# A graph layer on one core: the dense and the picked edges' steps of each stage moved a group of gathers apart

## What is computed

```python
src = node_feature[edge_src]
parts = [relu(node_feature)]
for t in range(3):
    msg = relu(src @ W_e[t].T + b_e[t])
    msg = where(edge_type == t, msg, 0)
    parts.append(segment_sum(msg, edge_dst, num_segments=N))
agg = concatenate(parts, axis=1)
updated[node] = agg[node] @ W_n[type of node].T + b_n[type of node]
x = layernorm(x + (updated + x))
```

## Time and profile before

| what | value |
|---|---|
| device time, 3 runs | 922.02 us median (919.35 to 922.12) |
| the profiled execution | span 1076.0 us from its first to its last instruction |
| PE busy | 771.1 us, 72% |
| DVE busy | 683.5 us, 64% |
| POOL busy | 671.4 us, 62% |
| ACT busy | 149.6 us, 14% |
| mean granted clock of PE | 0.872 |
| main loop: first gather, last gather | 107.01 us, 1049.44 us |

### The profile page before, as it was taken

One profiled execution on the slowest core, in us unless ns is written; L12 is line 12 of the kernel. 1 busy time (PEld: TensorE's weight loads), 2 busy tenths in 40 slices (PEclk: granted clock), 3 DMA queues, 4 the chain that ended last, 5 costly groups with the idle time before them and its releaser, 6 DMA issues. The chain is left out here.

```text
span 1076.0 us, 13097 instructions
## 1 busy us (share of the span) xinstructions
PE 771.1 (72%) x4200; PEld 611.8 (57%) x4200; DVE 683.5 (64%) x1539; ACT 149.6 (14%) x397; POOL 671.4 (62%) x718
## 2 busy tenths in 40 slices
PE   5574267777778778777676686888787786778866
PEld 3242156666666566566555565666566565566654
DVE  7997866666555656656566565656656654465645
ACT  2264101101101101100110110011011001111101
POOL 7776655666566666665666665666666666665660
PEclk9697578978898998998999988989888978898898
DMA  7476312422222223223223223223223233132320
GB/s 219 135 256 190 81 50 60 86 72 67 78 80 75 71 77 85 72 70 89 71 70 93 74 67 91 71 67 96 72 67 108 71 105 90 45 93 70 87 57 16
DMA packets 65777, 94.03 MB, mean 87 GB/s; under 512 B 16497, under 2 KB 49233, under 8 KB 65711
## 3 DMA queue, kind: packets, MB, share of 16 engines
q0 software_dynamic: 22432, 45.99, 17.2%
q1 hardware_dynamic: 40577, 43.14, 13.0%
q10 hardware_dynamic: 2702, 4.08, 1.3%
HBM read 80.23 MB, written 12.92 MB: 87 GB/s over the span
## 5 line engine op out<-in xcount | busy, mean ns | idle before, releaser
L619 POOL DMA_INDIRECT tab<-message_table,idx_t x630 | 594.3, 943 | 353.0 <-issue 170.4
L1116 DVE TENSOR_TENSOR work<-key_t,ps 128x378 f32<-128x378 f32 (+1 forms) x180 | 109.5, 610 | 253.1 <-remote 133.0
L1516 PE MATMUL ps<-work,tab 128*128 128x126 f32 x1260 | 197.4, 304 | 35.4 <-DVE acc L1125 20.6
L1516 PEld LDWEIGHTS ps<-work,tab 128*128 128x128 f32 x1260 | 183.3, 219 | 50.3 <-DVE acc L1125 25.5
L1546 PE MATMUL ps<-we_t,order_f 128*128 128x128 f32 x540 | 115.4, 368 | 123.2 <-DVE order_f L1204 84.1
L1546 PEld LDWEIGHTS ps<-we_t,order_f 128*128 128x128 f32 x540 | 93.3, 255 | 135.6 <-DVE order_f L1204 88.8
L1595 PE MATMUL ps<-wn_t,stage 128*128 128x384 f32 x294 | 104.6, 493 | 0.0
L1204 DVE TENSOR_TENSOR order_f<-ps,dst_raw 128x768 f32<-128x768 f32 x45 | 43.1, 957 | 71.7 <-remote 56.7
L615 POOL DMA_INDIRECT xg<-in_x,esrc_t x67 | 71.0, 1060 | 23.9 <-issue 17.7
L1595 PEld LDWEIGHTS ps<-wn_t,stage 128*128 128x128 f32 x294 | 56.3, 193 | 39.7 <-issue 3.1
L747 ACT ACTIVATE dense_f<-ps 128x256 f32<-128x256 f32 x45 | 17.2, 383 | 432.7 <-PE ps L1548 228.8
(11 more groups left out here) (231 smaller groups left out, 952.2 us busy)
## 6 DMA issues: line engine op xcount, KB each, us to landing
tab<-message_table,idx_t POOLq DMA_INDIRECT x630
message_table<-tab SPq DMA_DIRECT2D x24, 384.0 KB
dst_raw<-dense_types SPq DMA_DIRECT2D x45, 192.0 KB
wn_raw<-message_table SPq DMA_DIRECT2D x22, 384.0 KB
src_wide<-dense_lists SPq DMA_DIRECT2D x45, 128.0 KB
xg<-in_x SPq DMA_DIRECT2D x11, 256.0 KB
work<-in_x ACTq DMA_DIRECT2D x10, 256.0 KB
out<-xg SPq DMA_DIRECT2D x10, 256.0 KB
```

Of the source, the lines that this page charges most:

```text
L619: pool.indirect_dma_start(msg[:, slot, :], None, table, bass.IndirectOffsetOnAxis(ap=rows, axis=0)).then_inc(signal, 16)
L1116: dve.tensor_tensor(hot[:, first:first + n, :].rearrange("p c (t w) -> p c t w", w=WIN), keys.broadcast_to((P, n, T, WIN)), iota_win.rearr ...
L1516: ins = pe.matmul(sums_bank(nth), msg[:, column, :], hot[:, column, :], start=(c == 0), stop=(c == n - 1))
```

## The change

The dense and the picked edges' steps are spread over the stage, so that a group of gathers lies between one engine's step and the next engine's answer. The main parts:

- `dense_turn(j+1)` goes from the end of stage j to behind the sum of group 1; DVE makes its one-hots a group earlier, and masks after group 2. `dense_make(j)` stays behind the sum of group 0 (its mask is now made in stage j-1).
- `dense_sum(j)` is cut in two: side 0 behind the sum of group 2, side 1 behind the sum of group 3. From stage 2 to 43 their results go to spare columns of the two `AGG` banks (`D_SUM_AT`), in place of the bank `DENSE_PS`.
- The picked edges' sum goes to spare columns of the second `AGG` bank (`E_SUM_AT`) and has no turn of its own. `early_make` moves one stage later, behind the sum of group 0, `early_select` behind group 1, `early_sum` behind the sum of group 3.
- Because a bank now holds several sums, DVE waits for all of them before it adds the group's (`add_group`); all adds count on one semaphore, `added`, with a table of their order (`adds_of`).
- `finish_h(j-2)` is done at the end of stage j, where before it was done as `finish_h(j-3)` after group 1 of stage j; the two-step finish of the extra tiles goes over two stages.
- SP loads the dense edges' data ahead of the self rows, and the first batch of tiles is two in place of one.

```diff
@@ constants @@
-E_XT_PS, E_MSG_PS = 5, (6, 7)
+E_MSG_PS, E_XT_AT = (6, 7), T * D
+E_SUM_AT, D_SUM_AT = P, 2 * P
+PEELED_DENSE = 2
@@ order of the adds @@
+        def adds_of(j):
+            if j == 0:
+                return ["g0", "g1", "g2", "g3"]
+            if j == 1:
+                return ["g0", "g1", "p0", "p1", "g2", "g3", "e", "d0", "d1"]
+            if j == NI - 1:
+                return ["g0", "g1", "g2", "d0", "d1", "g3"]
+            return ["g0", "g1", "g2", "d0", "g3"] + (["e"] if j <= NE else []) + ["d1"]
...
@@ DVE, stage 1 @@
+            def iteration_one():
+                bases_of = load_bases(1, True)
+                dense_mask(0)
...
+                dve.wait_ge(group_summed, NG + 2)
+                one_hot(2, 1)
+                add_group(1, 1, bases_of[1])
+                first_of = load_bases(0, False)
+                for side in range(SETS):
+                    dense_add(0, side, first_of[2 * side], added_by(1, "p" + str(side)))
+                early_select(0)
+                self_types()
+
+                dve.wait_ge(group_summed, NG + 3)
+                one_hot(2, 2)
+                add_group(1, 2, bases_of[2])
+                dense_mask(1)
+                dense_hot(1)
...
+                dense_onehot(2)
+                dense_mask(2)
@@ DVE, stages 2 to 43 @@
+                dve.wait_ge(group_summed, NG * j + 3)
+                one_hot(j + 1, 2)
+                dve.wait_ge(d_summed, SETS * j + 1)
+                add_group(j, 2, bases_of[2])
+                dense_add(j, 0, bases_of[0], added_by(j, "d0"))
+                dense_mask(j + 1)
...
+                dve.wait_ge(group_summed, NG * j + 4)
+                one_hot(j + 1, 3)
+                dve.wait_ge(d_summed, SETS * j + 2)
+                if early:
+                    dve.wait_ge(e_summed, j)
+                add_group(j, 3, bases_of[3])
...
@@ PE, stage 1 @@
+                sum_group(1, 2)
+                dense_make(1)
+
+                sum_group(1, 3)
+                early_sum(0)
+                early_turn(1)
+                for side in range(SETS):
+                    dense_sum(1, side)
+                spread_types()
+                dense_turn(2)
@@ PE, stages 2 to 43 @@
+                sum_group(j, 0)
+                if j <= NE:
+                    early_make(j - 1)
+                dense_make(j)
...
+                sum_group(j, 1)
+                dense_turn(j + 1)
+
+                sum_group(j, 2)
+                dense_sum(j, 0)
+                finish_linear(j - 2, first=j == 2)
+                finish_turn(j - 1, j - 1, loads)
...
+                sum_group(j, 3)
+                dense_sum(j, 1)
+                if j <= NE:
+                    early_sum(j - 1)
+                if j < NE:
+                    early_turn(j)
+                place_selfs(j - 1, j - 1)
```

More of the change, by code:

```diff
@@ L66 @@
 FIN = 2
-BEHIND = 2
+PEELED_DENSE = 2
 WIN = 42
@@ L1366, in _ @@
             dve.wait_ge(acc_zeroed, 1 + 1 + 1 + 1 + 8 + 8)
[L1367 to L1369 removed]
+            iteration_zero()
+            iteration_one()
+            for j in range(2, NI - 1):
+                iteration(j, extra_of(j), extra_of(j - 1))
                 if j == BAD_AT - 1:
@@ L1549, in dense_make, with dense_sum @@
                 ins.then_inc(d_made, 1)
-            def dense_sum(j):
+            def dense_sum(j, side):
                 pe.wait_ge(d_ready, j + 1)
                 pe.wait_ge(d_hot, j + 1)
-                for side in range(2):
-                    ins = pe.matmul(dense_sums(side), dsel[:, side, :], dhot[:, side, :], start=True, stop=True)
-                ins.then_inc(d_summed, 1)
+                pe.matmul(dense_sums(j, side), dsel[:, side, :], dhot[:, side, :], start=True, stop=True
+                          ).then_inc(d_summed, 1)
             def spread_types():
@@ new lines, in iteration_zero, with iteration_one @@
+            def iteration_zero():
+                sum_group(0, 0)
+                early_turn(0)
+                for g in range(1, NG):
+                    sum_group(0, g)
+                dense_keys()
+                dense_turn(0)
+            def iteration_one():
+                sum_group(1, 0)
+                early_make(0)
+                dense_make(0)
+                sum_group(1, 1)
+                for side in range(SETS):
+                    dense_sum(0, side)
+                finish_turn(0, 0, 1, first=True)
+                dense_turn(1)
+                sum_group(1, 2)
[3 more added lines that the diff above has]
+                early_turn(1)
+                for side in range(SETS):
+                    dense_sum(1, side)
+                spread_types()
+                dense_turn(2)
@@ new lines, in last_iteration @@
+            def last_iteration(j):
+                sum_group(j, 0)
+                dense_make(j)
+                finish_turn(ORDER[KE], KE, 2, 1)
+                sum_group(j, 1)
+                finish_linear(j - 2)
+                finish_turn(j - 1, j - 1, len(BATCHES))
+                sum_group(j, 2)
+                for side in range(SETS):
+                    dense_sum(j, side)
+                place_selfs(ORDER[KE], KE, 1)
+                linear_open(KE, 1)
+                place_selfs(j - 1, j - 1)
+                linear_open(j - 1)
+                sum_group(j, 3)
+                linear_types(j - 1, 0)
+                linear_types(KE, 1)
@@ L1694, in batches_up_to @@
                 return sum(first <= tile for first, _ in BATCHES)
-            iteration(0, True, False)
-            dense_keys()
-            dense_turn(0)
-            for j in range(1, NI - 1):
-                iteration(j, j < NE, extra=j - EXTRA_AT if EXTRA_AT <= j < EXTRA_AT + KE else None,
-                          loads=batches_up_to(j - 1))
-            iteration(NI - 1, last=True)
-            linear_types(KE, 1)
+            iteration_zero()
+            iteration_one()
+            for j in range(2, NI - 1):
+                iteration(j, batches_up_to(j - 1), extra_of(j), extra_of(j - 1))
+            last_iteration(NI - 1)
             pe.wait_ge(ctl_set, 1)
```

438 lines of the change are left out of this document (182 added, 256 removed).

## The result

| | before | after |
|---|---|---|
| device time, median | 921.79 us (917.42 to 924.42, 16 runs) | 923.78 us (921.27 to 929.51, 16 runs) |
| ratio to before | | 1.0036 (1.0020 to 1.0051) |
| the same, timed again later | 920.29 us (35 runs) | 924.23 us (12 runs), 1.0040 (1.0019 to 1.0061) |
| span of the profiled execution | 1076.0 us; a second one 916.8 us | 924.7 us; a second one 924.0 us |

The change makes the kernel 0.36 to 0.40% slower, about 3.5 us. The forecast was 920.5 and no measurable change; slower by over 0.3% had 0.20. The time lies in the range given, but the likeliest case had the wrong sign.

The account below looks back on a forecast made before the run. The prediction took POOL's nearly back-to-back gather issue to bound the timed kernel. Its terms summed as 922.0 − 1 + 0 + 3 − 3.5 = 920.5 us, own range 915 to 926, with a wider range from 900 to 927.

Parts of the forecast that it names:

- The bound: Whole timed loop: POOL issues gathers nearly back to back, 3.4 us of waits left; the profile's stage waits come with profiling.
- Rival A: POOL's gathers: timed pitch shorter than 1.248 us, so stage waits remain and the change takes them; 896.5 to 905.5 us, chance 0.26.
- Rival B: Stage loop: profile at face value, POOL's waits of 127.8 us scale to 109.5 and go; 812 us, chance 0.04.
- 107.0 + 785.0 + 26.6: Profile's time ahead of the first gather, 629 gather pitches, and time from the last gather's start: 918.6 us.
- Step 1: PE's waits for mask, esel and finish_linear, 4.9 us a stage, all go; hidden beside POOL when timed, so −1 us.
- Step 2: Shared PSUM banks: DVE waits for all sums, likeliest some 0.3 us twice a stage, covered by its spare time; cost 0.
- step 3: dense_turn and early_make moved on PE, dense-edge loads moved ahead on SP; busy times hold, cost 0.
- Step 4: Stages 1 to 2: the sum of group 3 slides behind dense_make(1), later waits absorb part; bounds +1.0 and +5.5, taken +3 us.
- Step 5: Last stage: a tile finished and mask made a stage earlier, removing PE's variance wait; 0 to 4.82 us, taken −3.5.

Follow-up runs that it names:

- a_start: The changed kernel with both stage-1 steps put back (a_order) and DVE's self_types moved to the end of stage 0: 918.59 us, ratio 0.9975 to before.
- b_start: The kernel before with only DVE's self_types moved from stage 1 to the end of stage 0: 919.11 us, ratio 0.9966.
- b_again: The kernel before, unedited, profiled a second time: span 916.8 us, median 918.6 us (1 run).
- a_back: a_order plus, in the last stage, the extra tile's place_selfs and linear_open a group earlier on PE: 920.86 us, ratio 0.9993 to before.
- after_again: The changed kernel, unedited, timed and profiled again: 924.23 us, ratio 1.0040 to before.
- b_turn: The kernel before with one step of the change alone, dense_turn(2) ahead of the sum of group 0 of stage 2: 924.35 us, ratio 1.0037.
- a_s13: The changed kernel with the sum of group 3 of stage 1 put back ahead of dense_make(1) on PE: 924.72 us, ratio 1.0053 to before.
- a_turn2: The changed kernel with dense_turn(2) put back behind the sum of group 0 of stage 2: 923.74 us, again 923.10; ratios 1.0049 and 1.0032 to before.
- a_order: The changed kernel with both put back, group 3's sum ahead of dense_make(1) and dense_turn(2) behind stage 2's group-0 sum: 922.16 us, ratio 1.0025 to before.

## Why the prediction was wrong

*The bound.* Right for the stages: POOL is at its floor there at 922, and the profile's 127.8 us of waits don't exist in the timed runs. The second profile of before and the two runs with fewer gathers show it. Rival A (a shorter pitch) is out: the pitch is 1.249 to 1.252 in the thirteen undisturbed traces with all 630 gathers. Rival B too. But that 107.0 + 785.0 + 26.6 came within 3.4 us of the median was luck. The undisturbed ends are 100.7 and 13.8 us, 19.1 shorter, and POOL waits 16.9 us over its gaps, all of it ahead of stage 5 (6.24 us at 132.84 and 7.03 at 165.77 above all): 100.7 + 785.4 + 16.9 + 13.8 = 916.8. The two errors hid each other. It is these 17 us at the start, taken for 3.4, from which a_start and b_start have their gain.

*Step 1, the waits in a stage.* Right in kind, with sizes read from the odd execution. Undisturbed, PE of before waited for `esel` and the mask 9.1 us in 20 stages, 0.5 a stage and not 3.9. The rows for 300 to 650 us of b_again:

```profile
PE ps L1516 <- DMA tab<-message_table,idx_t: 47.1, 46, 2.3
PE ps L1506 <- DVE esel L1170: 8.3, 11, 1.6
PE ps L1546 <- DVE order_f L1204: 0.8, 2, 0.4
```

and of after:

```profile
PE ps L1575 <- DMA tab<-message_table,idx_t: 62.8, 56, 3.3
PE ps L1575 <- DVE acc L1248: 2.8, 3, 1.0
PE ps L1594 <- DVE first_wide L1219: 2.2, 3, 1.0
```

Both kernels' PE waits above all for gathers. What it was freed of went into more waiting for POOL (62.8 for 47.1). The −1 was 0: from 200 us on POOL of before had no wait left to lose (3.0 us in ten gathers, all ordinary gaps). The test that the prediction set, a profiled span of 950 to 980 us and a median that hardly moves, came out in kind: 924.7 us, with POOL's waits at 3.9 where under 30 was asked.

*Step 2, the shared banks.* Right. DVE's waits in the same stretch of after:

```profile
DVE work L1135 <- PE ps L1575: 54.9, 34, 4.0
DVE acc L1146 <- PE ps L1558: 5.7, 20, 0.3
```

The wait for the picked sum ahead of the add of group 3 is 0.28 us a stage (5.7 in 20), the 0.3 that was taken, and it is hidden. The Trainium skill's rule ("PSUM — Partial Sum Buffer", "PSUM bank collisions raise a hardware error ⚠️") of guarding by bank cost no time here: a_back has all its waits and takes 0.9993 of before. It also has step 3's moved steps and loads, whose cost of 0 holds to the same +0.7 and −2.0 us.

*Step 4, the start.* Its number was near, +3 for +4.0, its mechanism failed. The lower bound of +1.0 to +1.6 rests on what it put ahead of the sum of group 0 of stage 2: "four dense-sum matmuls and the first `dense_turn(2)`, 1.5 us". The dense-sum matmuls stood there before as well, and the 1.5 came from no row. What stands there in after is this (rows picked from the timeline of PE and DVE, stage 1 to 2):

```profile
158.11 0.94 DVE L1228 TENSOR_TENSOR order_f<-ps,dst_raw 128x768 f32<-128x768 f32 x1
159.11 1.65 PE L1607 MATMUL ps<-we_t,order_f 128*128 128x128 f32 x6 [7.24 <-DVE order_f L1228]
162.49 0.28 PE L1609 MATMUL ps<-be_rows,dmask 9*128 9x128 bf16 x1
162.70 2.07 PE L1575 MATMUL ps<-work,tab 128*128 128x126 f32 x8
164.81 0.68 DVE L1135 TENSOR_TENSOR work<-key_t,ps 128x504 f32<-128x504 f32 x1 [5.24 <-PE ps L1575]
168.02 0.81 DVE L1219 TENSOR_TENSOR first_wide<-src_wide,ps 128x640 f32<-128x640 f32 x1
168.98 1.35 PE L1594 MATMUL ps<-first_wide,tab 128*128 128x128 f32 x10 [2.26 <-DVE first_wide L1219]
170.17 1.28 PE L1594 MATMUL ps<-dense_f,tab 128*128 128x128 f32 x10
171.28 0.83 PE L1575 MATMUL ps<-work,tab 128*128 128x126 f32 x6
```

`dense_turn(2)` itself takes 2.3 us (3.7 in after_again, 4.4 in b_turn), and it waits for DVE's one-hots, which stand behind the add of group 3, the picked add, the self masks and two dense adds (164.81 to 168.83). Those wait for PE's sums, which all stand behind `dense_make(1)`. From the end of `dense_make(1)` to the sum are 8.5 us (162.77 to 171.28), in before 2.1 (160.87 to 162.94). With the sum of group 3 put back ahead of it they are still 9.1 (a_s13, 164.67 to 173.78), so the chain runs through the picked and the dense sums: PE to DVE to PE. The step looked at what PE issues and not at what DVE must have done first. Of the 6.7 us at stage 3, later waits gave back 2.7 and 4.0 stayed, so that the +3 came near by luck.

*Step 5, the end.* This failed, and by the greater size: −3.5 was forecast, and at a like clock (1.00) the end is 0.4 to 0.7 us shorter (13.1 in a_turn2 and 13.4 in a_start, for 13.8). PE's wait for the variance is there in the undisturbed before (2.69 us at 895.53), but 7.5 us ahead of the last gather's issue, so PE has made it good by then. The end of before:

```profile
895.53 0.32 PE L1586 MATMUL ps<-bn_parts,pick_parts 128*128 128x384 bf16 x1 [2.69 <-DVE mv L1246]
...
902.99 0.97 POOL L619 DMA_INDIRECT tab<-message_table,idx_t  x1 [0.30 <-issue]
...
905.96 1.05 PE L1516 MATMUL ps<-work,tab 128*128 128x126 f32 x8
```

and of after, where PE still does `linear_open` when the last gather is in:

```profile
909.75 0.95 POOL L641 DMA_INDIRECT tab<-message_table,idx_t  x1 [0.30 <-issue]
...
912.90 0.81 PE L1647 MATMUL ps<-wn_t,stage 128*128 128x384 f32 x2
...
913.54 1.05 PE L1575 MATMUL ps<-work,tab 128*128 128x126 f32 x8
```

The last two matmuls of a_turn2's last sum, where the clock was 1.00 and PE had to wait for the gather:

```profile
907.98 0.49 PE L1575 MATMUL ps<-work,tab 128*128 128x126 f32 x2 [0.26 <-DMA tab<-message_table,idx_t]
```

3.0 and 3.8 us lie between the last gather's start and the last sum. In a_turn2, with the order of after, the gather's landing ends the last wait, and the span ends 13.1 us behind its start: before was within 0.7 us of that, so no order of PE's steps ahead of the last sum could give the 3.5. The prediction named this case ("0, if the last gathers' landing and not PE sets the end") and took the other, though its own account had POOL as the bound everywhere else.

*The sum.* With −1, 0, +3 and −3.5 replaced by 0, 0, +4.0 and −0.7 to −0.4 (the end at a like clock) the traces give a loss of 3.3 to 3.6; with the ends as the two profiles have them, 13.8 and 14.95, it is 5.1. The ratios 1.0036 and 1.0040 give 3.3 and 3.7. At which clock the ends of the timed runs went isn't on record, so that the first figure meets them proves little. The wrong sign came from the end's term, which offset the start's: without it the prediction's sum is 924.0.

## What to carry to other kernels

Before anything is read from a profile, set its span against the timed median; where one engine's back-to-back work plus both ends nearly fills the median, gains elsewhere in the loop are slack and not time, and only its start and end can still move. There, a step moved ahead of another on one engine can cost all that its own inputs wait for on the others: follow each moved instruction's waits back to the queue behind which they stand. Leaving out some of the bounding engine's work (here 84 gathers) shows in one run what a change is worth beneath the bound: 23 us here, where the full kernel showed a loss of 3.5.

## What was unexpected of the hardware

The first profile of before was 154 us longer than the kernel's other runs, with PE's semaphores 2.7 to 3.3 us behind the recorded ends in the stage of the earlier trace rows; none of the other fifteen traces shows it, the second one of the same kernel among them. Its mean granted clock was 0.872, that of the second 0.926. What caused it was not found. PE did `dense_turn(2)` in 2.3 us in after and 3.7 in after_again, the same kernel; six matmuls of `dense_make` took 0.83 us or 1.65, a factor of two, as between the clock's two levels of 2.4 and 1.2 GHz. The granted clock of after from 159.1 to 162.7 us, behind 7.24 us in which PE stood idle, is the 0.50 in this row:

```profile
159.10:162.70 3.60, 3.59 (x15) 2.91 (x15) 0.47 (x1) 0.00 (x0) 0.00 (x0) 0.50 0.00 0
```

So a step at the start, behind a stretch in which PE stands idle, can cost twice its price in the loop, and a loss there can't be read from the loop's rows. The end is the same case: a_turn2 and a_order have the same last stage, and from the last gather on they took 13.1 and 16.6 us, at 1.00 and 0.50 in the 6 us ahead.
